# Moving the mask step ahead of the second values step in the projection stage of a two-layer cross-attention kernel

## What is computed

```python
x = x + _L0_xattn_ref(_layernorm(x), ctx, ctx, mask, ...)
# in it: qp = q @ Wq.T + bq, kp = k @ Wk.T + bk, vp = v @ Wv.T + bv, for 16 heads
scores = jnp.where(mask[:, None, :, :] == 0, -10000.0, qp.kp / 4)
x = x + _L0_ffn_ref(...); x = x + _L1_xattn_ref(...); x = x + _L1_ffn_ref(...)
```

## Time and profile before

| | |
|---|---|
| median of 3 runs | 1467.08 us (1466.75 to 1467.55) |
| the profiled execution | 1467.55 us, its span 1465.8 us |
| PE busy | 1307.9 us, 89% |
| DVE busy | 951.1 us, 65% |
| ACT busy | 849.5 us, 58% |
| POOL busy | 424.0 us, 29% |

### The profile page before, as it was taken

One profiled execution on the slowest core, in us unless ns is written; L12 is line 12 of the kernel. 1 busy time (PEld: TensorE's weight loads), 2 busy tenths in 40 slices (PEclk: granted clock), 3 DMA queues, 4 the chain that ended last, 5 costly groups with the idle time before them and its releaser, 6 DMA issues. The chain is left out here.

```text
span 1465.8 us, 21139 instructions
## 1 busy us (share of the span) xinstructions
PE 1307.9 (89%) x7327; PEld 643.9 (44%) x7327; DVE 951.1 (65%) x1647; ACT 849.5 (58%) x1489; POOL 424.0 (29%) x639
## 2 busy tenths in 40 slices
PE   8999945999999999999999989999995999970498
PEld 4655521333434434344455445544543444430387
DVE  5444415888787887877666687877762343996532
ACT  3544420777676776777755655555553446869432
POOL 0000000013543444345465433333331001648300
PEclk9999975999999999999999999999996999985699
DMA  8768656132342434423424553333210001316132
GB/s 293 248 252 289 239 166 188 45 96 60 94 122 75 121 84 121 123 80 88 111 83 120 154 153 88 96 112 96 57 39 17 0 0 43 133 82 258 43 101 86
DMA packets 87916, 170.75 MB, mean 116 GB/s; under 512 B 14586, under 2 KB 49157, under 8 KB 86277
## 3 DMA queue, kind: packets, MB, share of 16 engines
q1 hardware_dynamic: 87812, 169.42, 37.1%
HBM read 108.27 MB, written 60.31 MB: 115 GB/s over the span
## 5 line engine op out<-in xcount | busy, mean ns | idle before, releaser
L1202 DVE TENSOR_REDUCE b_neg_max<-b_score 128x1 f32<-128x512 f32 (+3 forms) x864 | 540.6, 663 | 218.6 <-PE b_score L765 108.5
L987 ACT ACTIVATE b_probs<-b_exp 128x512 f32<-128x512 f32 (+1 forms) x864 | 463.1, 582 | 307.5 <-PE b_exp L790 306.6
L765 PE MATMUL b_score<-b_k_stack,b_q_stack 97*128 97x512 bf16 (+3 forms) x1024 | 356.7, 352 | 34.1 <-issue 21.0
L790 PE MATMUL b_exp<-b_q_stack,b_k_stack 100*128 100x512 bf16 (+3 forms) x1024 | 345.0, 342 | 20.7 <-DMA b_q_stack<-b_max_rows 15.1
L811 PE MATMUL b_av<-b_probs,b_values 128*17 128x512 f32 (+3 forms) x2048 | 229.9, 521 | 3.6 <-POOL b_probs L1080 3.3
L765 PEld LDWEIGHTS b_score<-b_k_stack,b_q_stack 97*128 97x128 bf16 x1024 | 100.0, 98 | 271.0 <-DVE b_neg_max L1202 140.4
L1088 POOL CAST b_max_parts<-b_neg_max 128x16 bf16<-128x16 f32 x64 | 12.7, 198 | 506.6 <-DVE b_neg_max L1202 506.3
L790 PEld LDWEIGHTS b_exp<-b_q_stack,b_k_stack 100*128 100x128 bf16 x1024 | 100.4, 99 | 97.7 <-ACT b_probs L987 23.7
L1080 POOL TENSOR_SCALAR_AFFINE_SELECT b_probs<-b_probs 128x512 f32<-128x512 f32 x96 | 61.7, 643 | 184.6 <-ACT b_probs L987 184.3
L768 PE MATMUL b_score<-diag_qk,minus_big 128*128 128x128 bf16 x512 | 113.0, 221 | 0.0
L1746 PE MATMUL f_down<-f_w_downT,f_tmp 128*128 128x256 f32 x384 | 84.7, 384 | 4.6 <-DVE f_tmp L1423 4.6
(11 more groups left out here) (211 smaller groups left out, 1760.2 us busy)
## 6 DMA issues: line engine op xcount, KB each, us to landing
b_q_stack<-s_q SPq DMA_DIRECT2D x384, 64.0 KB
s_k<-a_part_k SPq DMA_DIRECT2D x48, 256.0 KB, 5.6
b_k_stack<-s_k SPq DMA_DIRECT2D x64, 192.0 KB
s_up<-f_up SPq DMA_DIRECT2D x6, 1536.0 KB, 5.1
s_va<-a_va SPq DMA_DIRECT2D x16, 544.0 KB, 5.0
b_values<-s_va SPq DMA_DIRECT2D x16, 544.0 KB, 4.3
a_mask_q<-mask_in SPq DMA_DIRECT2D x8, 1024.0 KB, 7.6
b_k_stack<-s_k SPq DMA_DIRECT2D x64, 128.0 KB
```

Of the source, the lines that this page charges most:

```text
L765: mm = pe.matmul(o, q, KS[half][0:R_MAX, h, 0:w], start=True, stop=causal or not general)
L790: mm = pe.matmul(o, k, QS[half][0:NSTACK, h, q0:T], start=True, stop=not masked)
L987: nc.scalar.activation(probs[kc][:, h0:h0 + m, q0:T], exp_bank[n % RINGS][:, 0:m * w].rearrange("p (h n) -> p h n", h=m), ACT.Exp).then_in ...
L1202: nc.vector.tensor_reduce(neg_max[u][:, qt, h0:h0 + m], score_bank[n % RINGS][:, 0:m * w].rearrange("p (h n) -> p h n", h=m), AX.X, ALU.ma ...
```

## The change

On DVE, for each batch b of 0 to 6, `mask_of(b + 1)` is moved from behind `values(b, 1, 1)` to ahead of `values(b, 1, 0)`, so also ahead of the copy of `XT`. Nothing is added or removed; the lists of the other engines stay the same.

```diff
                 if b == 0:
                     bias_split()
                     dve.wait_ge(one_landed, 64)
+                if b + 1 < NB:
+                    mask_of(b + 1)
                 values(b, 1, 0)
                 dve.wait_ge(x_turned, 2 * b + 2)
                 nc.vector.tensor_copy(XT[b % 2][:, 1, :], bank[(13 * b + 9) % 7][:, :]).then_inc(x_by_dve, 1)
                 values(b, 1, 1)
                 if b + 1 < NB:
-                    mask_of(b + 1)
                     moments(b + 1)
```

## The result

The kernel with the change takes 1494.23 us in the median (1493.85 to 1496.52, 4 runs) against 1467.32 (1466.75 to 1469.83, 4 runs) for the kernel before: a ratio of 1.0183, 95% interval 1.0166 to 1.0201, 26.9 us more. Its profiled execution took 1492.49 us, its span 1490.8; it was the fastest of the five executions of this kernel, so that it lies 24.9 us above the profiled execution of before, 2 us less than the medians do. The forecast was 1488.5, range 1479 to 1496.

The account below looks back on a forecast made before the run. PE was taken to bound the projection stage. Stalls of 14.6 us plus clock falls of 6.8 sum to 21.4, giving 1489.0 against the profiled 1467.55 and 1488.5 for the median (1467.08); range 1479 to 1496.

Parts of the forecast that it names:

- PE sets the pace: Projection stage: PE is busy for all of 23.30 us, DVE for 10.21, so any wait of PE adds in full.
- The last wait is the mask's landing: Moved step on DVE, batch 2: DVE arrives at 66.42, the mask lands at 72.44, 6.0 us later, after its other waits.
- The copy of `XT` decides: Of the DVE work behind the moved step, PE's q0 waits for this copy, which ends 4.75 us after the mask's landing.
- The size of the stalls, 14.60: PE before q0, batches 1 to 6: each stall is landing time + 4.79 - 9.80 (9.64 for mask 6), together 14.60 us.
- the signal to PE: From the end of the `XT` copy to PE's q0: estimated 0.04 us, bounds nothing and 0.2.
- Batch 0 costs nothing: Mask 1 is there by 21.51 and `XT` ends at 27.41, before q0's 28.20: no stall, 0.8 us to spare.
- The stores cost nothing: Stores of the values and k1 start 0.8 us later against PE but have some 12 us: nothing, upper bound 4.8.
- The clock, 6.8 from four falls: PE's clock halves for 3.40 us after four of six stalls, 1.70 us each: 6.8 us, bounds nothing and 10.2.
- the clock holds: Rival: stalls as worked out, but PE's dense work keeps the clock at full speed: 1481.7 us, chance 0.22.
- the wait is covered: Rival: the mask lands within 5.0 us of its issue, `XT` comes in time, time stays at 1467.1 us; chance 0.06.
- Feedback: Rival: later stores crowd the next loads, masks take 10.0 us, stalls are 4.99 each, six clock falls: 1507.2 us, chance 0.07.
- a faster kernel: Rival: the moments and next normed x come up to 3.45 us earlier and free PE: up to 20.7, to 1446.4; chance 0.02.

Follow-up runs that it names:

- early load: The changed kernel, with SP asking for the next mask two places sooner, ahead of the next context and the wait for q0's split: 1467.38 us, ratio 1.0002.
- the reduction put back: The changed kernel with only the mask's comparison in the new place, its reduction back ahead of the moments: 1470.01 us, ratio 1.0019.
- the stalls filled: The changed kernel with 12 unneeded matmuls on PE ahead of its wait for `XT` in batches 1 to 6: 1483.41 us; same fill in the kernel before: 1481.09.
- mask first: The changed kernel with SP issuing the next batch's mask ahead of its context: 1471.10 us, ratio 1.0028.
- half the fill: The changed kernel with 6 unneeded matmuls on PE ahead of its wait for `XT` in batches 1 to 6: 1486.20 us, ratio 1.0130.
- mask last: The changed kernel with SP issuing the next batch's mask behind the load of x: 1507.02 us, ratio 1.0274.

## Why the prediction was right, step by step

**PE sets the pace.** Right, and shown in both directions: 2.5 us more PE work in six batches of the kernel before made its stage 15.0 us longer, and 3.45 us of DVE work moved into DVE's gap cost nothing when the mask was there (early load).

**The last wait is the mask's landing.** Right: 5.95 to 6.55 us of DVE idle before the mask step in batches 1 to 6, "about 6" by the prediction, and none in batch 0. Moving the landing both ways moved the stalls with it.

**The copy of `XT` decides.** Right: with the step behind the copy the time is that of before.

**The size of the stalls, 14.60.** Somewhat small: 15.9 as the profile counts idle time, 16.6 by the stage with the clock held. Two parts of the formula landing + 4.79 - 9.80 were off. The landings of masks 2 to 7 were 7.4, 7.4, 7.3, 7.5, 7.9 and 7.5, so that of mask 6 was not again the short 6.5 on which one stall of 1.65 had been built. And the signal to PE was the mis-sized term, taken as 0.04 with 0.2 as its upper bound, and it lay above that bound: the copy ends at 79.59 + 0.68 = 80.27 and the first matmul starts at 80.53, 0.26 later; it is 0.26 in all six batches. Against 0.04 that is 6 x 0.22 = 1.3 us. The row between them shows that PE's weight load, too, began only at 80.49, 0.22 after the end of the copy:

```profile
80.49 0.30 PEld L242 LDWEIGHTS a_bank<-a_xT,wq 128*128 128x128 f32 x2 [2.99 <-issue]
```

The same excess of 0.22 in each of six batches is most of what the kernel with the reduction put back had over its expectation (3.1 against 1.5).

**Batch 0 costs nothing.** Right: the copy began at 27.21 and ended 0.8 us before PE's q0 at 28.73, with DVE's mask step at 23.17 and not waiting, although this time mask 1 took 11.0 us to land. The prediction has a slip here: DVE comes to the mask at 22.72, and the sum starts from 22.66, which gives 27.41 in place of 27.47. Against the 28.20 of before, the measured end of the copy, 27.89, would have left 0.3 us and not 0.8.

```profile
27.21 0.68 DVE L486 COPY a_xT<-a_bank 128x512 f32<-128x512 f32 x1
```

(Batch 0's q0 itself began 0.53 later than before. I take that for no effect of the change: over the ten kernels traced it begins between 27.25 and 28.73.)

**The stores cost nothing.** Right as far as it can be seen: with the stalls filled, no batch is longer than the fill and the wait for the copy explain.

**The clock, 6.8 from four falls.** The mechanism was right, the size too small: five of six stalls, and 20.5 us slow instead of 13.6. By the filled stall it is worth 8.9 us in the profiled executions, by PE's busy time 9.6. The step that was off is the count of falls and the taking of one stretch of 3.40 us for each: batch 5's fall lasted 6.8 us. The rule of the Trainium skill that was weighed there ("TensorE: Matmul & The Clock Gate", section "HAM oscillation — how this bites in real kernels"), by which idle times this short leave the clock alone, doesn't hold in this trace: the clock fell after waits of 2.47 to 3.06 us.

**The rivals.** That the clock holds is refuted by the windows at 0.51. That the wait is covered would need a landing within 5.0 us; the shortest in the changed kernel was 7.3. Feedback and a faster kernel did not show: landings had a median of 7.5, before 7.6.

Added up for the profiled executions: 16.6 for the stalls, 8.9 for the clock, 0.5 for the later start, less 1.0 in the other stages, is 25.0; predicted were 14.6 and 6.8, 21.4 together. Both terms came out too small, so neither error hid the other. The medians are 26.9 us apart, and the remaining 1.9 are not in these two executions.

## What to carry to other kernels

Before an instruction is moved up in the list of an idle engine, look up when each thing that it waits for is there: a gap as long as the instruction's own time is no room if its data lands later, and then everything behind it in that engine's list is late too. Compare landing plus work with the moment at which the full engine wants the first result behind it; here 7.5 + 5.0 against 9.8 us, and two lines higher in the loading queue, or two lines lower in DVE's, made the same move free. A stall of TensorE costs more than its length when the clock falls in it: here more than half as much again (9.6 us on top of 15.9).

## What the runs showed of the hardware

The clock fell in stalls of 2.5 to 3.1 us in the middle of otherwise gapless matmuls, and not in waits of up to 1.5 us (mask first, half the fill), though in the kernel before it fell after one of 1.56 us among less dense work; it did not fall in every stall of 2.5 us either (batch 1, 2.53). What it does then is not a matter of the stall alone: in the twelve falls of three kernels (five in the changed one, one with half the fill, six with the mask last) it was down for 6.8 us in the six that came 0.6 to 1.9 us before PE went on, and for 3.4 us in the six that came less than 0.6 us before that or after it.

72 matmuls that compute nothing made the changed kernel 10.8 us faster, by keeping the clock up through stalls that were there anyway. In a kernel whose stalls can't be removed that is worth a try.

From the end of a DVE copy to the first fp32 matmul that waits for it are 0.26 us when PE stands still (all six batches of the changed kernel).

Exchanging the order of two loads of 1 MB and 0.5 MB on the queue took PE's waits from 15.9 to 4.3 us, and the landings of the 1 MB from 7.3 to 7.9 us after their issue to 5.6 to 6.9: the time at which a transfer landed depended on what stood ahead of it, not on its own size alone.
